# Query, key and value projections of the first attention block from split 16 bit operands, with GpSimd writing the low parts of queries and keys

## What is computed

```python
h = _layernorm(x, axis=-1) * (1 + ca) + sa
q = jnp.einsum('bnd,de->bne', h, Wq) + bq
k = jnp.einsum('bnd,de->bne', h, Wk) + bk
v = jnp.einsum('bnd,de->bne', h, Wv) + bv
scores = jnp.einsum('bne,bme->bnm', q, k)
weights = softmax(scores, axis=-1)
x = x + ga * jnp.einsum('bnm,bme->bne', weights, v)
...                    # second part of block 0, then block 1: not touched
```

## Time and profile before

| what | value |
|---|---|
| median of 3 runs | 4325.37 us |
| the profiled execution, its own time | 4327.25 us |
| its span in the profile | 4325.6 us |
| PE busy, share of the span | 3880.3 us, 90% |
| DVE busy | 3372.1 us, 78% |
| ACT busy | 2553.8 us, 59% |
| POOL busy | 1169.8 us, 27% |
| the stage of the change, first instruction to last | 29.87 to 126.89 us |

### The profile page before, as it was taken

How to read it: one execution, slowest core, us unless ns; L and a number is a source line. 1 busy time by engine, 2 the same in 40 slices (tenths; PEclk the granted TensorE clock), 3 DMA queues, 4 the chain that set the end, 5 groups by cost and what they waited for, 6 DMA issues and landing times. The chain is left out here.

```text
span 4325.6 us, 95192 instructions
## 1 busy us (share of the span) xinstructions
PE 3880.3 (90%) x38484; PEld 2197.5 (51%) x38484; DVE 3372.1 (78%) x5530; ACT 2553.8 (59%) x3441; POOL 1169.8 (27%) x958
## 2 busy tenths in 40 slices
PE   7999999669989969998986999999999999867996
PEld 4788888535555535555553332332333333434764
DVE  5688888779985479985787899999998978585454
ACT  3566666545554345653423777787888887635563
POOL 1122221277861067761141000000000000013552
PEclk9999999889999989999997999999999999977998
DMA  1011110133320033320063000000000000032444
GB/s 62 5 40 31 40 31 18 44 70 62 64 47 28 0 70 65 64 49 8 0 140 65 9 9 2 9 2 2 9 2 2 9 2 9 4 99 74 90 106 103
DMA packets 290198, 167.00 MB, mean 39 GB/s; under 512 B 204596, under 2 KB 281096, under 8 KB 289288
## 3 DMA queue, kind: packets, MB, share of 16 engines
q1 hardware_dynamic: 267176, 125.49, 13.5%
q0 software_dynamic: 13440, 21.24, 2.7%
q10 hardware_dynamic: 9184, 14.68, 1.1%
HBM read 77.81 MB, written 38.58 MB: 27 GB/s over the span
## 5 line engine op out<-in xcount | busy, mean ns | idle before, releaser
L2211 DVE TENSOR_REDUCE s_tops<-ps 128x2 f32<-128x1024 f32 (+3 forms) x1152 | 1250.2, 1131 | 143.4 <-PE ps L2097 104.0
L2180 ACT ACTIVATE s_weights<-ps 128x1024 f32<-128x1024 f32 (+3 forms) x1152 | 1092.7, 952 | 343.2 <-PE ps L2110 192.6
L2132 PE MATMUL ps<-s_weights,v_flat 128*32 128x256 f32 (+1 forms) x8704 | 692.8, 390 | 7.1 <-ACT s_o_t L2186 6.0
L2091 PE MATMUL ps<-keys,s_q 48*128 48x512 f16 (+3 forms) x2304 | 434.7, 375 | 48.1 <-DVE s_tops L2211 27.2
L2110 PE MATMUL ps<-s_q,keys 50*128 50x512 f16 (+3 forms) x2304 | 434.5, 374 | 45.9 <-DVE s_tops L2211 33.6
L2247 POOL CAST s_shift<-s_minus_top 128x16 f16<-128x16 f32 x32 | 6.3, 196 | 1428.2 <-DVE s_minus_top L2218 1428.2
L583 PE MATMUL ps<-a_qt,a_kt 128*128 128x256 f16 x3072 | 375.3, 273 | 3.8 <-POOL s_ones L538 3.8
L2110 PEld LDWEIGHTS ps<-s_q,keys 50*128 50x128 f16 x2304 | 112.2, 93 | 511.6 <-issue 252.5
L1173 PE MATMUL ps<-attention_w,la_yt 128*128 128x512 f16 x1152 | 289.9, 399 | 37.9 <-DMA la_yt<-la_y_parts 30.4
L583 PEld LDWEIGHTS ps<-a_qt,a_kt 128*128 128x128 f16 x3072 | 300.8, 98 | 40.3 <-POOL s_ones L538 4.2
L1248 ACT ACTIVATE la_weights<-ps 128x1024 f32<-128x1024 f32 x124 | 126.9, 1023 | 296.4 <-PE ps L1163 296.4
(11 more groups left out here) (371 smaller groups left out, 7209.4 us busy)
## 6 DMA issues: line engine op xcount, KB each, us to landing
ex_whole<-in_L_ffn_w_dram ACTq DMA_DIRECT2D x14, 1024.0 KB
qk_parts<-a_parts SPq DMA_DIRECT2D x64, 128.0 KB, 4.1
keys<-qk_parts SPq DMA_DIRECT2D x48, 128.0 KB, 5.2
s_q<-qk_parts SPq DMA_DIRECT2D x48, 128.0 KB, 4.8
x<-in_x_dram SPq DMA_DIRECT2D x8, 512.0 KB, 9.4
attention_w<-attention_split SPq DMA_DIRECT2D x2, 2048.0 KB, 9.0
la_table<-in_rotary_dram SPq DMA_DIRECT2D x64, 64.0 KB, 2.1
a_table<-in_rope_dram POOLq DMA_DIRECT2D x8, 512.0 KB, 5.7
```

Of the source, the lines that this page charges most:

```text
L2091: mm = pe.matmul(m.ps[:, bank, 0:width], b.q[rows(half, KEY_PARTS * L1_DH), place % 2, pair, t * P:(t + 1) * P], m.keys[rows(half, KEY_PAR ...
L2132: mm = pe.matmul(m.ps[h * QUAD:(h + 1) * QUAD, OUT, begin:end], m.v_flat[:, first:first + QUAD], weights[:, a % 2, h, begin:end], start=(k ...
L2180: act.activation(weights[:, a % 2, 2 * pair:2 * pair + 2, skip:CHUNK], m.ps[:, bank:end + 1, skip:CHUNK], ACT.Exp).then_inc(s["exp"], 1)
L2211: dve.tensor_reduce(tops[:, u % 2, :, i % 2, t, c], m.ps[:, bank:end + 1, 0:width], AX.X, ALU.max).then_inc(s["max"], 1)
```

## The change

Weights and activations are each split into a high and a low float16 part. The weights are first multiplied by 64 (`SCALE`), and the outputs are divided by 64 again. Each float32 product becomes three float16 products, high x high, high x low and low x high (`TERMS`). ACT makes the high parts of the weights at the start and of `a_ht` in every chunk; DVE makes the low ones. For q and k, DVE no longer writes the low part: it writes the whole value to a new two-buffered tile `a_whole` in float32, and POOL subtracts the high part from it. The normalisation of chunk c+2 moves on DVE from ahead of the q and k outputs of chunk c to between those and its v outputs. PE may overwrite a bank of q or k when `a_whole` is written.

```diff
-                def outputs(c, u):
-                    dve.wait_ge(s["w_in"], 16 * LOADS)
+                def split():
+                    for n in range(3):
+                        dve.wait_ge(s["w_high"], n + 1)
+                        dve.scalar_tensor_tensor(w[n][:, 1, :, :], w_whole[n][:, :, :], SCALE, w[n][:, 0, :, :], ALU.mult, ALU.subtract).then_inc(s["w_low"], 1)
+
+                def ht_low(c, u):
+                    need(dve, s["mm"], 6 * (c - 1))
+                    for k in range(KD):
+                        need(dve, s["ht_high"], KD * c + k + 1)
+                        dve.tensor_tensor(halves[:, u, 1, k, :], ht[:, u, k, :], halves[:, u, 0, k, :], ALU.subtract).then_inc(s["ht_low"], 1)
+
+                def outputs(c, u, between=None):
                     for n in range(2 * KD):
                         need(dve, s["high"], 2 * KD * c + n + 1)
-                        to, b = (m.qt, bcol["q"]) if n < KD else (m.kt, bcol["k"])
-                        dve.scalar_tensor_tensor(to[:, n % KD, 1, bass.ts(c, CHUNK)], m.ps[:, 2 + n, :], b[:, n % KD:n % KD + 1],
-                                                 to[:, n % KD, 0, bass.ts(c, CHUNK)], ALU.add, ALU.subtract).then_inc(s["ev"], 1)
+                        need(dve, s["ev"], 2 * KD * c + n - 2 + 1)
+                        b = bcol["qk"[n // KD]]
+                        dve.tensor_scalar(whole[:, n % 2, :], m.ps[:, 2 + n, :], 1 / SCALE, b[:, n % KD:n % KD + 1], ALU.mult, ALU.add).then_inc(s["whole"], 1)
+                    if between:
+                        between()
                     for b in range(2):
...
-                two_ahead_in_pairs(dve, CHUNKS, norm, outputs)
+                norm(0, 0)
+                norm(1, 1)
+                dve.wait_ge(s["w_in"], 16 * LOADS)
+                split()
+                ht_low(0, 0)
+                with dve.Fori(0, CHUNKS // 2 - 1) as k:
+                    for u in range(2):
+                        ht_low(k * 2 + u + 1, 1 - u)
+                        outputs(k * 2 + u, u, lambda: norm(k * 2 + u + 2, u))
+                ht_low(CHUNKS - 1, 1)
+                outputs(CHUNKS - 2, 0)
+                outputs(CHUNKS - 1, 1)
...
             def _(act):
-                credit(act, s["ht"], s["high"], s["v_high"])
+                credit(act, s["ht"], s["ht_high"], s["high"], s["v_high"])
+                act.wait_ge(s["w_in"], 16 * LOADS)
+                for n in range(3):
+                    act.activation(w[n][:, 0, :, :], w_whole[n][:, :, :], ACT.Copy, scale=SCALE).then_inc(s["w_high"], 1)
...
+                    for k in range(KD):
+                        need(act, s["ht"], KD * c + k + 1)
+                        act.copy(halves[:, u, 0, k, :], ht[:, u, k, :]).then_inc(s["ht_high"], 1)
...
                 def low(c, u):
+                    for n in range(2 * KD):
+                        to = m.qt if n < KD else m.kt
+                        need(pool, s["whole"], 2 * KD * c + n + 1)
+                        pool.tensor_tensor(to[:, n % KD, 1, bass.ts(c, CHUNK)], whole[:, n % 2, :], to[:, n % KD, 0, bass.ts(c, CHUNK)],
+                                           ALU.subtract).then_inc(s["ev"], 1)
...
                 def products(c, u):
-                    pe.wait_ge(s["w_in"], 16 * LOADS)
-                    need(pe, s["ht"], KD * (c + 1))
+                    pe.wait_ge(s["w_low"], 3)
+                    need(pe, s["ht_low"], KD * (c + 1))
+                    terms = [(k, p, q) for k in range(KD) for p, q in TERMS]
                     for n in range(2 * KD):
-                        need(pe, s["ev"], 2 * KD * (c - 1) + n + 1)
+                        need(pe, s["whole"], 2 * KD * (c - 1) + n + 1)
                         o = n % KD
-                        for k in range(KD):
-                            mm = pe.matmul(m.ps[:, 2 + n, :], w["qk"[n // KD]][:, k, o * P:(o + 1) * P], ht[:, u, k, :],
-                                           start=(k == 0), stop=(k == KD - 1))
+                        for i, (k, p, q) in enumerate(terms):
+                            mm = pe.matmul(m.ps[:, 2 + n, :], w[n // KD][:, p, k, o * P:(o + 1) * P], halves[:, u, q, k, :],
+                                           start=(i == 0), stop=(i == len(terms) - 1))
```

More of the change, by code:

```diff
@@ L325, in attention0_projections @@
         LOADS = 6
-        w = {n: sb(f"w{n}", [P, KD, D]) for n in "qkv"}
+        SCALE = 64.0
+        TERMS = (0, 0), (0, 1), (1, 0)
+        w_whole = [sb(f"w{n}", [P, KD, D]) for n in "qkv"]
+        w = [sb(f"w{n}_parts", [P, 2, KD, D], F16) for n in "qkv"]
+        halves = sb("ht_parts", [P, 2, 2, KD, CHUNK], F16)
+        whole = sb("whole", [P, 2, CHUNK])
         bcol = {n: sb(f"b{n}", [P, KD]) for n in "qk"}
@@ L332, in attention0_projections @@
         v = sb("v_whole", [P, 2, 2, D])
-        with stage(nc, "a0", "w_in", "normed", "turned", "ht", "mm", "high", "ev", "v", "v_high", "v_low") as (block, s):
+        with stage(nc, "a0", "w_in", "w_high", "w_low", "normed", "turned", "ht", "ht_high", "ht_low", "mm", "whole", "high", "ev", "v", "v_high", "v_low") as (block, s):
             @block.sync
             def _(sp):
-                for n in "qkv":
-                    sp.dma_start(w[n][:, :, :], a[f"W{n}"].rearrange("(k p) e -> p k e", p=P)).then_inc(s["w_in"], 16)
+                for n, whole_w in zip("qkv", w_whole):
+                    sp.dma_start(whole_w[:, :, :], a[f"W{n}"].rearrange("(k p) e -> p k e", p=P)).then_inc(s["w_in"], 16)
                 for n in "qk":
@@ L345, in _ @@
             def _(dve):
-                credit(dve, s["normed"], s["ev"], s["v"])
+                credit(dve, s["normed"], s["ht_low"], s["whole"], s["v"])
                 def norm(c, u):
@@ L380, in high @@
                         act.activation(to[:, n % KD, 0, bass.ts(c, CHUNK)], m.ps[:, 2 + n, :], ACT.Identity,
-                                       bias=b[:, n % KD:n % KD + 1]).then_inc(s["high"], 1)
+                                       bias=b[:, n % KD:n % KD + 1], scale=1 / SCALE).then_inc(s["high"], 1)
                     for b in range(2):
@@ L386, in scaled @@
                 def scaled(c, u):
+                    need(act, s["ht_low"], KD * (c - 1))
                     need(act, s["mm"], 6 * (c - 1))
@@ L396, in _ @@
             def _(pool):
-                credit(pool, s["v_low"])
+                credit(pool, s["v_low"], s["ev"])
                 pool.memset(m.v[:, :, D:D + V_ONES], 1.0)
                 def low(c, u):
+                    for n in range(2 * KD):
[3 more added lines that the diff above has]
+                                           ALU.subtract).then_inc(s["ev"], 1)
                     for b in range(2):
@@ L432, in products @@
                         for j in range(2):
-                            for k in range(KD):
-                                mm = pe.matmul(m.ps[:, 6 + b, j * D:(j + 1) * D],
-                                               ht[:, u, k, (2 * b + j) * P:(2 * b + j + 1) * P], w["v"][:, k, :],
-                                               start=(k == 0), stop=(k == KD - 1))
+                            for i, (k, p, q) in enumerate(terms):
+                                mm = pe.matmul(m.ps[:, 6 + b, j * D:(j + 1) * D], halves[:, u, q, k, (2 * b + j) * P:(2 * b + j + 1) * P],
+                                               w[2][:, p, k, :], start=(i == 0), stop=(i == len(terms) - 1))
                         mm.then_inc(s["mm"], 1)
```

5 lines of the change are left out of this document (2 added, 3 removed).

## The result

The changed kernel takes 4337.92 us in the median of 9 runs (4331.91 to 4340.86); the kernel before, run between them, 4324.70 (4316.49 to 4335.72). The ratio is 1.0029, with a 95% interval of 1.0019 to 1.0039: some 13 us slower. A second set of 12 runs of the same kernel gave 1.0016 (1.0007 to 1.0025), some 7 us. Both intervals lie above 1, so it is slower; they have 1.0019 to 1.0025 in common, 8 to 11 us. The profiled execution has a span of 4336.3 us, before 4325.6. One run of the kernel before, beside one_term, dead_parts, four and best, was a slow one with 9340.91 us and is in none of the ratios.

What follows compares the result with a forecast made beforehand. PE alone was taken to set the stage's pace. Head +4.9, first chunk -1.2, five rounds +3.5, chunk 6 to 7 -2.5, tail -1.4, clock +3 made +6 us: 4331.5 us, range 4320 to 4342.

Steps and rivals of the forecast that it cites:

- Head: Stage start: ACT's weight casts wait for the last load, so products begin at 40.8 instead of 35.9 us, +4.9.
- PE's work: PE's products and transposes in a chunk of the stage: 8.7 us at full clock instead of 11.2.
- The ring: Stage rounds: waits through DVE, ACT and POOL from one normalisation's end to the next, 11.9 us a round against PE's 11.2.
- Collision: DVE and POOL: a normalising instruction waits for POOL's running one; normalisation of 4 tiles stretched to some 2.3 us.
- rival B: Stage rounds shorter, 11.1 us, as normalisation passes ahead of POOL's fourth subtraction or ways are shorter; 4323 us, chance 0.24.
- The Trainium skill's contention: DVE beside POOL: VectorE instructions in two-port mode or with two SBUF inputs are held up by GpSimd.
- Clock: PE idles 3.2 us a round; half clock in first products and some rounds, mostly absorbed, +3 us (0 to +9).
- The stage's sum: All stage terms: +3.3 us at full clock, +3 for the clock, +6 together.
- The rest unchanged to a few us: Kernel outside the changed stage: unchanged to a few us in the profile after.
- within 0.3%: Whole kernel: time within 0.3% of before, chance 0.82; faster by more 0.04, slower by more 0.14.

Runs made afterwards that it cites:

- one_term: Changed kernel with only the high x high product of the three for each pair; ratio 1.0015 to the kernel before.
- dead_parts: Changed kernel with float32 products from the unsplit weights, the 16 bit parts made but not read; ratio 1.0029 to the kernel before.
- four: Changed kernel with four buffers of a_whole instead of two; ratio 1.0017 to the kernel before.
- best: Changed kernel, weights unscaled, DVE writing q/k low parts from PSUM, normalisation before q/k outputs, chunk 0 scaled and cast during weight loads; ratio 0.9974 to before.
- three: Changed kernel with chunk 0 scaled and cast during weight loads, normalisation before q/k outputs, four a_whole buffers; ratio 1.0003 to the kernel before.
- low_dve: Changed kernel with unscaled weights, DVE writing q/k low parts from PSUM, POOL's four subtractions for q/k gone; ratio 0.9987 to the kernel before.
- norm_first: Changed kernel with the normalisation of chunk c+2 ahead of chunk c's q and k outputs on DVE; ratio 1.0004 to the kernel before.

## Why the prediction was right, and where not

- *Head*, forecast +4.9 with the first product at 40.8: 40.33 measured, 4.5 later. Right. The terms as listed add up to 40.6.
- *PE's work*, forecast 8.7 us a chunk: 8.88 at the full clock with ends, 8.70 where PE is full (three, best). Right.
- *The ring*, forecast 11.9 a round: 11.4. Right in kind; one_term shows that PE is not in it, low_dve and norm_first that POOL and the normalisation are. The size was 0.5 too long. The terms as listed even add up to 12.1 and not to 11.9. Against the round from 63.45, the normalisation's end, to 74.93, each stretch was a little shorter: v outputs and last v cast 2.0 instead of 2.1, scalings and first cast 2.0 instead of 2.16, POOL's first two subtractions 2.2 instead of 2.3, and from POOL's third to the normalisation's end 3.1 instead of 3.35.
- *Collision*, a normalising instruction waits for POOL's running one: right, 2.29 us beside 1.37 without POOL. The fourth POOL subtraction does get in between, as forecast; rival B said it would not.
- *The Trainium skill's contention* (GPSIMD Engine Reference, Key points), of VectorE in a two-port mode: the trace agrees that the two engines get in each other's way (in which mode the instructions ran, it does not show), 3.22, 2.29 and 1.37 us for the same four instructions by how much of POOL's work lies over them. The factor of about two that the Trainium skill gives for GpSimd's two-input work (same page, section 4.1, Engine selection) is not what a subtraction takes here: 1.16 to 1.17 us beside 0.69 is 1.7.
- *Clock*, forecast +3 us, mostly absorbed in the rounds. In the rounds shown it was at half for 3.4 us, from the end of one to the start of the next (0.95 and 0.90 in the last two windows); these took 11.93 and 11.24, so 0.3 us was lost in the two. The first chunk's products cost most: the 24 for q and k took 7.9 us (40.33 to 48.21) instead of 5.2 (53.15 to 58.33), and chunk 1 came 12.8 us after chunk 0 where 10.2 were forecast. And in chunk 6, behind the rounds, the clock was at half again: 12 products took 4.44 us, and chunk 7 came 9.5 us later instead of 7.8. Together the clock cost some 4.5 us and not 3.

```profile
110.45 4.44 PE L467 MATMUL ps<-a_ht_parts,a_wq_parts 128*128 128x512 f16 x12
```

```profile
110.45:113.85 3.40, 3.40 (x11) 1.26 (x9) 0.68 (x2) 3.40 (x7) 2.21 (x2) 0.53 0.00 0
```

- *The stage's sum*, forecast +6: +3.8. The five rounds took 57.3 us and not 59.5, the head 0.4 less, and from the last chunk's products to the end 2.5 us were saved and not 1.4; against that the clock cost 1.5 more. That the sum is off by only 2 us is in part luck: errors of both signs.
- *The rest unchanged to a few us*: this step failed. The stage explains 4 us of 7 to 13. Behind the stage the changed kernel's local attentions of block 0 took 1054.0 us instead of 1043.2; with 16 bit products they take 6.5 us more in the mean of nine profiles. Why is open. The forecast of +6 for the total came out too small in the first set of runs and right in the second, and for the wrong sum: 2 us too much in the stage, some 6 missing behind it. That the total was near is luck. The time lay in the range; the change was forecast as most likely within 0.3%, and it is just at that edge.

## What to carry to other kernels

When one engine is full and its work is cut, follow the written orders of the other engines round to where they began before counting the gain: if the sum of one turn is longer than the new work, the gain is gone, and no engine looks full. Work that is moved to GpSimd can cost the vector engine where the two overlap: here four normalising instructions took 1.4 us with GpSimd idle and 2.3 and 3.2 beside its subtractions, while outputs that read PSUM kept their 0.75. Put such instructions where GpSimd idles. Before taking a wait list's name for a wait, look whether the engine named had long been done. Here moving one call brought 8 us of the stage, while two more buffers brought 2 to 3.

## What the runs showed that was not expected

A change in 2% of the span costs as much behind it as in it, and most of that in one place, the local attentions of block 0. How PE's clock can carry something there is to be seen in the second layer's, where before and after run the same instructions. PE's timeline of the changed kernel, and below it that of the kernel before at the same place:

```profile
1591.87 0.47 PE L1180 MATMUL ps<-la_kt,la_qt 64*128 64x256 f16 x4 [1.60 <-DMA la_qt<-la_parts]
1592.28 2.74 PE L1212 MATMUL ps<-attention_w,la_yt 128*128 128x512 f16 x6
```

```profile
1577.99 0.39 PE L1141 MATMUL ps<-la_kt,la_qt 64*128 64x256 f16 x4 [0.78 <-DMA la_qt<-la_parts]
1578.31 1.47 PE L1173 MATMUL ps<-attention_w,la_yt 128*128 128x512 f16 x6
```

PE waited 1.60 us for a load instead of 0.78, the clock fell to half, and the next six products took 2.74 us instead of 1.47. The window rows of the two:

```profile
1592.00:1595.40 3.40, 3.40 (x13) 1.31 (x10) 2.76 (x10) 0.00 (x0) 3.32 (x2) 0.51 0.27 58
```

```profile
1578.00:1581.40 3.40, 3.40 (x32) 1.85 (x33) 2.92 (x11) 0.38 (x1) 3.32 (x2) 1.00 0.30 63
```

The six products are slower for the clock, as the two rows show; that the longer wait brought the clock down is only argued from the order of events. Nor does it show why all nine profiles with 16 bit products should be slow in this stretch, by 6.5 us in the mean, and the five with float32 products in none; no run here settles that, and it stays open. A next step would be to compare the waits and the granted clock of this stretch window by window in several profiles of one pair of kernels.
